# Values of four steps in one run, both score halves together, and the column maxima turned by a product in a fused attention and FFN layer

## What is computed

```python
xn = layernorm(x)
q_c = (xn @ Wq_down @ Wq_up)   # 128 heads x 4     k_c, v_c likewise from xn @ Wkv_down
q_r = xn @ Wq_rope             # 128 heads x 64    k_r = xn @ Wk_rope  (one for all heads)
scores = (q_c . k_c + q_r . k_r) / sqrt(68)
s = softmax(scores) @ v_c @ Wo
g = silu(ffn(xn))              # silu(w1 path) * w3 path, then w2, each with rank-2 terms
out = x + s * g
```

## Time and profile before

| | us |
|---|---|
| median of 3 runs | 1966.09 (1965.21 to 1967.59) |
| the profiled execution | 1965.53 |
| its span, first to last instruction | 1963.4 |
| TensorE busy | 1931.3 (98%) |
| VectorE busy | 1388.5 (71%) |
| ScalarE busy | 1054.9 (54%) |
| GpSimd busy | 471.9 (24%) |

### The profile page before, as it was taken

One profiled execution on the slowest core, in us unless ns is written; L12 is line 12 of the kernel. 1 busy time (PEld: TensorE's weight loads), 2 busy tenths in 40 slices (PEclk: granted clock), 3 DMA queues, 4 the chain that ended last, 5 costly groups with the idle time before them and its releaser, 6 DMA issues.

```text
span 1963.4 us, 37694 instructions
## 1 busy us (share of the span) xinstructions
PE 1931.3 (98%) x12464; PEld 1505.0 (77%) x12464; DVE 1388.5 (71%) x1645; ACT 1054.9 (54%) x1543; POOL 471.9 (24%) x790
## 2 busy tenths in 40 slices
PE   6999999999999999999999999999999999999999
PEld 5777877777787777778777777777877777775666
DVE  8688767676776767777676777767777676687655
ACT  5656555555555555555555555555555555554222
POOL 5323121212212121212121222222121213111221
PEclk9999999999999999999999999999999999999999
DMA  7612121111212121212111111212121211234331
GB/s 237 210 39 61 29 42 37 39 37 35 45 27 50 28 48 27 50 29 42 35 39 37 39 39 30 47 29 50 25 50 28 46 31 40 47 85 131 108 102 54
DMA packets 133995, 107.97 MB, mean 55 GB/s; under 512 B 52366, under 2 KB 97918, under 8 KB 133886
## 3 DMA queue, kind: packets, MB, share of 16 engines
q1 hardware_dynamic: 133918, 107.38, 23.2%
q10 hardware_dynamic: 32, 0.01, 0.0%
HBM read 52.80 MB, written 27.26 MB: 41 GB/s over the span
## 4 chain that ended last, share of the span: by engine, by line
PE 94%; DVE 2%; SPq 2%; DMA 1%; issue 1%; ACT 0%; POOL 0%; DVEq 0%; POOLq 0%; ACTq 0%
PE pj L999 35%; PE st L968 24%; PE sx L985 12%; PE ob L944 12%; PE ap L1603 2%; PE sx L952 1%; PE yp L1637 1%; PE zp L1637 1%; PE gp L1544 1%; PE zp L1590 1%; PE gp L1569 1%; DVE mx L906 0%; PE up L1544 0%; PE gp L1545 0%; PE gp L1546 0%
## 5 line engine op out<-in xcount | busy, mean ns | idle before, releaser
L906 DVE TENSOR_REDUCE mx<-sx 128x4 f32<-128x1024 f32 x512 | 627.0, 1225 | 428.0 <-PE sx L985 410.0
L887 ACT ACTIVATE probs<-st 128x1024 f32<-128x1024 f32 x512 | 513.0, 1025 | 162.3 <-PE st L968 161.7
L848 ACT ACTIVATE slot<-pj 64x512 fp32r<-64x512 f32 x512 | 303.4, 592 | 424.1 <-PE pj L999 417.7
L782 POOL CAST k<-kc 64x512 fp32r<-64x512 f32 x256 | 167.7, 655 | 1054.1 <-PE st L968 1053.8
L968 PE MATMUL st<-slot,k 89*128 89x512 f32 x1024 | 418.3, 409 | 1.7 <-DMA slot<-mrow 1.7
L968 PE MATMUL st<-slot,krlh 128*128 128x512 f32 x1024 | 408.5, 399 | 0.0
L999 PE MATMUL pj<-xh,wh 128*128 128x512 f32 x1024 | 401.8, 392 | 0.9 <-DVE slot L916 0.8
L999 PE MATMUL pj<-xh,wl 128*128 128x512 f32 x1024 | 401.2, 392 | 0.0
L999 PE MATMUL pj<-xl,wh 128*128 128x512 f32 x1024 | 400.0, 391 | 0.0
L916 DVE TENSOR_TENSOR slot<-pj,slot 64x512 fp32r<-64x512 f32 x512 | 352.8, 689 | 17.3 <-ACT slot L848 1.2
L985 PEld LDWEIGHTS sx<-k,slot 88*128 88x128 f32 x2048 | 314.7, 190 | 49.4 <-issue 3.6
(11 more groups left out here) (180 smaller groups left out, 1293.1 us busy)
## 6 DMA issues: line engine op xcount, KB each, us to landing
w_stage<-in_Wq_rope SPq DMA_DIRECT2D x64, 256.0 KB, 3.1
c_scratch<-stage SPq DMA_DIRECT2D x32, 256.0 KB, 3.1
c_in<-c_scratch SPq DMA_DIRECT2D x128, 64.0 KB, 2.0
o_scratch<-o_sb SPq DMA_DIRECT2D x128, 64.0 KB, 2.1
k<-kc SPq DMA_DIRECT2D x128, 48.0 KB
slot<-kc SPq DMA_DIRECT2D x256, 24.0 KB
k<-kx SPq DMA_DIRECT2D x128, 48.0 KB
slot<-kx SPq DMA_DIRECT2D x256, 24.0 KB
```

The costliest lines, as they stand in the source:

```text
L782: nc.gpsimd.tensor_copy(k1[0:64, s, :, :].rearrange("p a n -> p (a n)"), krh[:, bp * CH:(bp + 1) * CH]).then_inc(k_ready, 1)
L848: nc.scalar.activation(slot1[0:64, (k - 1) % NS, e, :, :], pj[64 * e:64 * e + 64, :].rearrange("p (a n) -> p a n", a=2), ACT.Copy).then_in ...
L887: nc.scalar.activation(probs[:, k % NS, kt], st[:, kt], ACT.Exp, scale=SCALE).then_inc(exp_done, 1)
L906: nc.vector.tensor_reduce(mx[:, p, lo:lo + 4], sx[:, :, :].rearrange("p a (b k) -> p (a b) k", b=2), axis=AX.X, op=ALU.max).then_inc(red_d ...
```

## The change

In the steady order a step is now: scores x8 (in odd steps with the product for the maxima between the two halves), row scores x4, 9 products of the projection, row scores x4, the last 3 products of the projection. In the first step of a turn the values of four steps, x64, come between the scores and the row scores. The maxima are turned by a product with a rounded identity (`unit`, 128 x 128, `mx` now of the rounded type too) into the second half of the bank `ob`, so that a row score no longer waits for `mrow`; instead one turn's transposition waits for `o_evac`. `content_hi` and `content_lo` move from the third step of a turn (s == 2) to its first (s == 0), for the first turn too. SP issues the next turn's loads ahead of the step's own content rows. VectorE takes the first row maximum ahead of its copy of `slot1`, except in a turn's first step. The end of attention (`drain`) and the FFN's preparations are reordered.

```diff
@@ SP
-            if s == 0:
-                hold(sp, passed, ct_hi, at.turn(k) + 1)
-                hold(sp, passed, ct_lo, at.turn(k) + 1)
-                hold(sp, passed, ct_copy, 2 * at.turn(k) + 2)
@@
                 if at.live(k) and k < STEPS:
-                    if k > 1 or not at.first:
-                        load_content(sp, at, k)
                     if k % NS == 0:
+                        if k or not at.first:
+                            content_split(sp, at, k)
                         load_v(at, k)
                         if at.live(k + NS):
                             next_content(at, k)
+                    if k > 1 or not at.first:
+                        load_content(sp, at, k)
@@ ScalarE
-                if s == 1 and at.live(k - 6):
-                    act.wait_ge(av_done, at.step(k) - 5)
-...
-                    nc.scalar.activation(o_sb[:, :], ob[:, 0, :], ACT.Copy).then_inc(o_evac, 1)
-                if k % 2 and at.live(k - 3) and k - 3 < STEPS:
-...
+                if at.first and k == NS:
+                    nc.scalar.activation(unit[:, :], ident[:, :], ACT.Copy).then_inc(unit_ready, 1)
+                if at.last and s == 0:
+                    tail(act, k, True)
+                ending = at.last and k > STEPS
+                if k % 2 and at.live(k - 3) and not ending:
+                    max_row(at, k - 3, ob[0:16, 1, 0:128])
                 if at.live(k - 4) and k - 4 < STEPS:
-                    if k % 2 == 0:
-                        exponentials(at, k - 4, 0)
+                    exponentials(at, k - 4, 0)
+...
                     exponentials(at, k - 4, 1)
-                if k % 2 == 0 and at.live(k - 3) and k - 3 < STEPS:
-                    exponentials(at, k - 3, 0)
-                if s == 2 and k < STEPS and at.live(k + 2):
+                if s == 0 and k < STEPS and at.live(k + NS):
                     content_hi(k // NS + 1, at.turn(k) + 1)
+                if s == 0 and at.live(k - 5):
+                    act.wait_ge(av_done, at.step(k) - 4)
+...
+                    nc.scalar.activation(o_sb[:, :], ob[:, 0, :], ACT.Copy).then_inc(o_evac, 1)
@@ VectorE
-                if at.live(k - 1) and k <= STEPS:
+                    if k % NS:
+                        maxima(at, k - 1, 0)
                     nc.vector.tensor_copy(slot2[0:64, s], slot1[0:64, s]).then_inc(s2_done, 1)
-                    maxima(at, k - 1, 0)
-                if k % NS == 2 and k < STEPS and at.live(k + 2):
+                    if k % NS == 0:
+                        if at.last:
+                            tail(dve, k, True)
+                        maxima(at, k - 1, 0)
+                if k % NS == 0 and k < STEPS and at.live(k + NS):
                     content_lo(k // NS + 1, at.turn(k) + 1)
@@ TensorE
+                pe.wait_ge(red_done, 2 * at.step(k) + 4)
+                if k % NS and k < 3 * NS and (k > NS or not at.first):
+                    pe.wait_ge(o_evac, at.turn(k))
+...
+                    last = nc.tensor.matmul(row, mx[:, (k // 2) % 2, :], unit[:, :], start=True, stop=True)
@@
-                    if k % 2 == 0 and at.live(k - 2):
-                        pe.wait_ge(mrow_ready, at.g * (STEPS // 2) + k // 2)
@@ project
                 for c in range(KD):
+                    if c == KD - 1 and at.live(k - 1):
+                        row_scores(at, k - 1, 1)
@@ body
+                if at.last and k >= STEPS:
+                    drain(at, k)
+                    return
+                if at.live(k - 4):
+                    scores(at, k - 4, 0)
+                if k % 2 and at.live(k - 3):
+                    transpose_maxima(at, k - 3, ob[0:16, 1, 0:128])
+                if at.live(k - 4):
+                    scores(at, k - 4, 1)
+                if k % NS == 0 and at.live(k - 2 * NS):
+                    turn(at, k - 2 * NS)
+                if at.live(k - 1):
                     row_scores(at, k - 1, 0)
+                project(at, k)
+
+            def turn(at, k):
+                for i in range(NS):
+                    values(at, k + i, 0 if i else NS)
+
+            def drain(at, k):
+                if k == STEPS:
+                    turn(at, 8)
+                    row_scores(at, 15, 0)
+                    for kt in range(2):
+                        scores(at, 12, kt)
+                    row_scores(at, 15, 1)
+                    for kt in range(2):
+                        scores(at, 13, kt)
+                    transpose_maxima(at, 14, sx[0:16, 0, 0:128])
+                if k == STEPS + 1:
+                    values(at, 12, 2)
+                    values(at, 13, 0)
+                if k == STEPS + 2:
+                    for v in (14, 15):
+                        for kt in range(2):
+                            scores(at, v, kt)
+                    values(at, 14)
+                    values(at, 15)
@@ VectorE's preparations for the FFN
+        if waiting:
+            if k == 12:
+                dve.wait_ge(den_loaded, 16)
+                nc.vector.reciprocal(den1[0][:, :], den1[0][:, :]).then_inc(recip, 1)
+            if k == 16:
+                weight_o_lo(dve, 0)
+            return
-        if k in (15, 16):
-            n = k - 15
-            dve.wait_ge(den_loaded, 16)
-            rows = den1[0][:, 256 * n:256 * n + 256]
-            nc.vector.reciprocal(rows, rows).then_inc(recip, 1)
```

More of the change, by code:

```diff
@@ L702, in load_content, with content_split @@
                              c[8 * s + 4 * e:8 * s + 4 * e + 4, 1:4, :].bitcast(F32)).then_inc(ct_in[s], 16)
+        def content_split(sp, at, k):
+            hold(sp, passed, ct_hi, at.turn(k) + 1)
+            hold(sp, passed, ct_lo, at.turn(k) + 1)
+            hold(sp, passed, ct_copy, 2 * at.turn(k) + 2)
         def first_content(sp):
+            content_split(sp, At(0, True, False), 0)
             for k in range(2):
@@ L880, in body, with max_row @@
                     refill(at.g, 3)
+            def max_row(at, k, row):
+                p = k // 2
+                act.wait_ge(mt_done, at.g * (STEPS // 2) + p + 1)
+                nc.scalar.activation(mrow[:, p % 2, :], row, ACT.Copy).then_inc(mrow_ready, 1)
             def exponentials(at, k, kt):
@@ L936, in values @@
                     pe.wait_ge(vx_filled, NS + 1)
-                if s == 0:
-                    if at.live(k - NS):
-                        pe.wait_ge(o_evac, at.turn(k))
+                if at.last and k == 3 * NS:
+                    pe.wait_ge(o_evac, at.turn(k))
                 for kt in range(2):
@@ L948, in values, with transpose_maxima @@
                 last.then_inc(av_done, 1)
-            def transpose_maxima(at, k):
+            def transpose_maxima(at, k, row):
                 pe.wait_ge(red_done, 2 * at.step(k) + 4)
-                nc.tensor.transpose(sx[0:16, 0, 0:128], mx[:, (k // 2) % 2, :], ident[:, :]).then_inc(mt_done, 1)
+                if k % NS and k < 3 * NS and (k > NS or not at.first):
+                    pe.wait_ge(o_evac, at.turn(k))
+                if at.first and k == 0:
+                    pe.wait_ge(pre.krl_done, NC)
+                    pe.wait_ge(pre.lora_raw_done, NC)
+                    last = nc.tensor.transpose(row, mx[:, 0, :].bitcast(F32), ident[:, :])
+                else:
+                    if at.first and k == 2:
+                        pe.wait_ge(unit_ready, 1)
+                    last = nc.tensor.matmul(row, mx[:, (k // 2) % 2, :], unit[:, :], start=True, stop=True)
+                last.then_inc(mt_done, 1)
             def scores(at, k, kt):
@@ L1024, in body @@
-                if k < STEPS:
-                    project(at, k)
-                if at.last and k == STEPS:
-                    for v in (k - 6, k - 5):
-                        values(at, v)
-                if at.live(k - 1) and k <= STEPS:
-                    row_scores(at, k - 1, 1)
-                if ending and k == STEPS + 1:
-                    transpose_maxima(at, k - 3)
+                project(at, k)
+            def turn(at, k):
+                for i in range(NS):
+                    values(at, k + i, 0 if i else NS)
@@ L1420, in vector_head, with weight_o_lo, vector_tail @@
             nc.vector.tensor_tensor(sl[:, cs], s_raw[:, cs], sh[:, cs], ALU.subtract).then_inc(sl_done, 1)
-    def vector_tail(dve, k):
+    def weight_o_lo(dve, n):
+        j = 2 * n
+        dve.wait_ge(wo_hi, n + 1)
+        nc.vector.tensor_tensor(wol[:, j:j + 2, :], wo_raw[:, j:j + 2, :], woh[:, j:j + 2, :],
+                                ALU.subtract).then_inc(wo_lo, 1)
+    def vector_tail(dve, k, waiting=False):
+        if waiting:
+            if k == 12:
+                dve.wait_ge(den_loaded, 16)
+                nc.vector.reciprocal(den1[0][:, :], den1[0][:, :]).then_inc(recip, 1)
+            if k == 16:
+                weight_o_lo(dve, 0)
+            return
         if k in (11, 14, 17):
```

98 lines of the change are left out of this document (40 added, 58 removed).

## The result

The changed kernel takes 1978.44 us, median of four runs (1976.12 to 1980.26), beside 1965.84 for the kernel before on the same chip: ratio 1.0062, 95% interval 1.0045 to 1.0079, 12.6 us slower. The prediction was 1972.6 us, slower, range 1955 to 1985. The profiled execution took 1976.84 us with a span of 1974.7, 11.3 more than the span before.

The account below looks back on a forecast made before the run. TensorE's own stream was taken as the bound (busy 400.00 of 400 us mid-attention). 8.8 + 1.3 - 2.6 - 1.9 - 2.5 + 3 + 0.4 = +6.5 us gave 1972.0 profiled, 1972.6 against the median; range 1955 to 1985.

Parts of the forecast that it names:

- The hold: First turn, step 0: ScalarE waits for c_in before copying the first pj, delaying the second projection; +8.8 us.
- The rival without a hold: First turn: SP's stores ahead of c_in had waited for something the change frees; 1962.5 us, chance 0.10.
- The half clock: After TensorE's stop in the first turn, some 3 us at half clock; +1.3 us, bounds 0 to 3.
- Steps 1 to 7: First group after the second projection: fewer waits for maxima and mrow, -2.6; values moved to step 8, -1.9 us.
- The loop: Steady turns: fewer value runs, turned products in the open, a pj wait; -0.04 us per turn, -2.5 over 62 turns.
- The strong rival: Loop gains far more: cheap turned product, projections at 2.73, pj wait covered; 0.34 less per turn, 1954 us, chance 0.18.
- the one with odd steps waiting: Loop: odd steps also wait, for pj and maxima; 0.3 us more per turn, +19, 1991 us, chance 0.17.
- FFN preparations: VectorE's additional pieces in both unrolled groups, in steps without values, delay TensorE; together +3 us, 0 to 6.
- the one wait that was spelled out: Last group, step 12: the 3.34 us reciprocal ahead of a row maximum makes TensorE wait 0.8 us.
- The end of attention: Reordered last stage, written out step by step: 22.4 us where it was 22.0, +0.4 us.

Follow-up runs that it names:

- the late first split: Changed kernel, but for the first turn alone the c_in rows are split at step 2, not step 0; 1966.01 us, ratio 1.001.
- three repairs: Late first split plus: numerator loads after the last mrow, 1965.64 us; first-group FFN pieces moved, 1965.25; both plus last-group weight loads moved, 1961.37.
- the third repair: Late first split plus first-group pieces moved, numerator loads after the last mrow, and last-group a2, one b13 set and w2 loads later; 1961.37 us, ratio 0.9984.

## Why the prediction was right, and where its terms were off

**The first turn: right, and shown from both sides.** The hold was priced at +8.8 and measured +8.9 in the changed kernel; +9.0 (14.49 against 5.52) when put into the kernel before alone, and absent when taken out of the change (5.54). ScalarE's row came at 83.06 and the second projection at 86.00, both some 0.7 ahead of the forecast; the first projection was 0.75 ahead too. The rival without a hold is refuted.

**The half clock: mis-sized.** +1.3, measured 2.2 by the kernel with the gap filled, within its bounds of 0 and 3. The restart in the earlier trace rows followed stops of 1 to 2 us and lasted 3.4 us; here the products are slow from 84.98 to 90.81, 5.8 us. The profile before had no stop of 10 us to read it from. The Trainium skill, "TensorE: Matmul & The Clock Gate", section The HAM clock gate, has the clock fall without activity and return after a spell of work; the trace agrees, with a granted clock of 0.57 around the stop and 1.00 when products fill it. The prediction put the term by that section nearer its upper bound, and there it was.

**Steps 1 to 7: mis-sized.** I took 2.6 + 1.9 = 4.5 us of gain; -1.0 - 2.2 = -3.2 was measured. TensorE's waits for the maxima in these steps did not all go: they fell from 2.6 us to 1.0, of which 0.8 stand ahead of one product for the maxima at 110.74. With them stand 0.3 for `pj` and 0.9 before row scores for which the profile shows no releaser. These 2.2 us are what the sum of pure step times left out; in the kernel before all waits of this stretch were 3.8.

**The loop: the terms right, the gain near nothing.** Predicted per turn -0.70 + 0.34 + 0.22 + 0.10 = -0.04, measured -0.01. Term by term, by the starts of the products: the 64 values are 0.33 dearer than what they stream (3.59 - 3.45 of streaming, 0.09 more in the last score, 0.10 more in the row scores), against 0.34, and a second run is 0.34 dearer; the two turned products add 0.12 and 0.13, against 0.22 together; the third step's projection is 0.07 late, against 0.10. These give -0.05. The turn that they predict is the shorter of the two values that the loop shows: the kernel with the late first split has 26.418, -0.06. In the longer one, 26.467, the step of the late projection has 5.79 us instead of 5.75 and the other three are nearly the same; that is most of the 0.04 that is missing. Streaming is what counts in values: they are 3.45 of 26.5 us, and that stays however they are grouped. The strong rival and the one with odd steps waiting are both refuted by 26.463. The turned product costs 0.12 to 0.13 and not 0.06. The 0.06 is what "TensorE: Matmul & The Clock Gate" of the Trainium skill, section Back-to-back issue gap, gives for an isolated product of 128 columns; in a stream with weight loads, it says, this counts too little. The trace agrees: the product's own start-to-start is 0.06, and the rest shows in the product behind it.

That VectorE needs the row scores ahead of the last three products was in the prediction, without a price. It is some 1.7 us per turn.

**FFN preparations: the sum right, the place wrong.** +3 predicted, 1.7 + 1.3 measured. That the sum came out is luck: no row priced it, the one wait that was spelled out is absent, and part of what was measured is no FFN preparation of VectorE but SP's queue. The step with the reciprocal did not wait 0.8 us for its maximum: the longest piece lies in a step of 10 us, which is long enough. What waited in the last group was the product for the maxima, 1.5 us, in the step where SP issued the content rows late. VectorE's timeline of the changed kernel there:

```profile
1700.56 0.69 DVE L914 TENSOR_TENSOR kc<-c_in,kc 64x512 fp32r<-64x512 f32 x1 [2.42 <-ACT kc L846]
1701.28 1.23 DVE L920 TENSOR_REDUCE mx<-sx 128x4 fp32r<-128x1024 f32 x1
```

`content_lo` stands ahead of the maximum and waits 2.42 us for ScalarE's part, and that for rows that SP issued only at 1696.1. I had costed SP's queue at nothing in the loop, which held, and had no term for it in the unrolled groups, where it also issues weights. With some of SP's weights moved away from that step, the 1.5 us are gone (the third repair).

**The end of attention: a wait left out.** +0.4, measured +1.9. The last row of maxima landed 7.2 us after its issue, where it took 3.8 before, and TensorE waits 1.93 for it. The kernel before had such a wait already:

```profile
1776.22 0.50 PE L968 MATMUL st<-slot,k 89*128 89x512 f32 x1 [1.75 <-DMA slot<-mrow]
```

The prediction wrote the new order of this stage out step by step. It agrees with the trace to 0.3 us up to the scores of steps 14 and 15, which it has 14.5 us into the stage; they start at 16.2, behind the row. With a transfer of 3.8 us, as before, the row would have been there in time. In the kernel before SP issues the numerator loads at 1763.8, 8.5 us ahead of that row, and the spread of the denominators at 1775.5, behind it; in the changed kernel they follow each other, just ahead of the row at 1782.7:

```profile
1773.80 2.60 SPq L1221 DMA_DIRECT2D num<-o_scratch  x4
1776.44 3.72 SPq L1216 DMA_DIRECT2D den<-r_scratch  x4
```

Taken away, the row lands in 4.5. The prediction named this stage's DMA issue by ScalarE but had no term for the transfer behind it.

**The total.** The spans differ by 11.3 us and the sum was 6.5; the 4.8 between them are 1.9 of the loop, 1.5 of the end of attention, 1.3 of steps 1 to 7 and 0.9 of the half clock, less 0.75 and 0.2 in stages that the change leaves alone. All but the last two went the same way.

**What stays open.** A turn of the new loop is 26.418 us in the trace of the kernel with the late first split and 26.467 in those of its three repairs, 2.7 us over the loop. It isn't a property of the kernel alone, since the changed kernel's trace has turns of both kinds; what selects it isn't shown. Differences of 0.05 us per turn between two traces are therefore not to be read as an effect of an edit. In the first group VectorE's pieces moved most of their wait with them; no kernel tried them outside it.

## What to carry to other kernels

Before an operation is moved forward in a hand-written pipeline, look at the first pass through it: where the loop has its input ready for a turn, the prologue may have to wait for a transfer, and all that stands behind it on its in-order engine waits too. One such placement cost 10 us in a kernel whose 56 looped turns gained 0.6 (3.1 in the trace with the shorter turn). And when the order of an engine changes near the end of a stage, read again what the DMA queues issue just ahead of the last small transfer.

## What the runs showed of the hardware

- A run of four-way tiled products costs 0.32 to 0.37 us beside its streaming, whether it has 32 or 64 products; a transposition behind it adds nearly nothing, between two score halves it costs 0.11.
- A rounded product with 128 moving columns takes 0.06 us from start to start, and the next product with other 128 columns of weights takes 0.28 instead of 0.23: no less than a transposition.
- An 8 KB transfer issued 2.5 us behind eight of 256 KB takes 7.2 us to land (6.8 to 7.6 in the eight traces with this order of issues). It takes 4.5 without them, and also 4.5 when four of them stand 6.3 us ahead of it.
- After a stop of 9.6 us nine products that cost 0.23 us each at full clock took 0.43 (the first 0.56); with 40 products in the stop they cost 0.23.
